# Who makes the remainders of the second expert weights: GpSimd's and VectorE's shares redrawn in a metaformer block

## The reference

```
x = x + conv_attention(layernorm(x))         # q, k, v; softmax along rows plus softmax along columns; Wo
t = layernorm(x) as 2048 tokens
expert of a token = argmax of softmax(t @ wg); its place = how many came before it; 256 places each
h = relu(dispatched[e] @ w1[e])              # 256 x 256 by 256 x 1024, eight experts
y = h @ w2[e]                                # 256 x 1024 by 1024 x 256
x = x + gate * y, put back at the token
```

## Time and profile before

| | before |
|---|---|
| median of 3 runs | 187.49 us (187.36 to 187.66) |
| the profiled execution | 187.47 us, its span 185.5 us |
| TensorE busy | 176.2 us, 95% of the span |
| VectorE busy | 142.3 us, 77% |
| GpSimd busy | 120.7 us, 65% |
| ScalarE busy | 113.6 us, 61% |

### The profile page before, as it was taken

One profiled execution on the slowest core, in us unless ns is written; L12 is line 12 of the kernel. 1 busy time (PEld: TensorE's weight loads), 2 busy tenths in 40 slices (PEclk: granted clock), 3 DMA queues, 4 the chain that ended last, 5 costly groups with the idle time before them and its releaser, 6 DMA issues.

```text
span 185.5 us, 3928 instructions
## 1 busy us (share of the span) xinstructions
PE 176.2 (95%) x1372; PEld 169.5 (91%) x1372; DVE 142.3 (77%) x394; ACT 113.6 (61%) x275; POOL 120.7 (65%) x156
## 2 busy tenths in 40 slices
PE   7999999999999999999999979999999999999980
PEld 7998999999989997779999969999999999999970
DVE  0697749889998899763557899699996998995820
ACT  3348776968859787715578990691953955827000
POOL 4267264787888988579237599538587196369552
PEclk9999999999999999999999999999999999999997
DMA  5897996731111329392999129257166192261010
GB/s 171 240 391 223 321 241 168 277 117 59 62 59 57 111 71 310 102 349 99 265 339 306 43 68 393 77 189 266 58 223 255 58 345 112 44 208 47 4 69 28
DMA packets 23860, 31.66 MB, mean 171 GB/s; under 512 B 2728, under 2 KB 20649, under 8 KB 23840
## 3 DMA queue, kind: packets, MB, share of 16 engines
q1 hardware_dynamic: 21264, 26.32, 43.9%
q0 software_dynamic: 1616, 4.24, 6.4%
q10 hardware_dynamic: 960, 0.85, 1.4%
HBM read 23.02 MB, written 8.55 MB: 170 GB/s over the span
## 4 chain that ended last, share of the span: by engine, by line
PE 70%; DVE 14%; ACT 4%; DMA 3%; issue 3%; POOL 3%; POOLq 1%; SPq 0%; DVEq 0%; ACTq 0%
PE banks_v L634 7%; PE banks_v L635 7%; PE banks_v L641 7%; PE banks_o L706 5%; PE bank_pT L634 4%; PE bank_pT L641 4%; PE bank_pT L635 4%; PE bank_q L641 3%; DMA sl<-in_x 3%; PE bank_s L641 3%; PE bank_q L634 3%; PE bank_q L635 3%; PE bank_s L634 3%; PE bank_s L635 3%; DVE qT_low L1165 2%
## 5 line engine op out<-in xcount | busy, mean ns | idle before, releaser
L984 ACT ACTIVATE w_high<-w_in_sb 128x1024 fp32r<-128x1024 f32 x22 | 22.9, 1058 | 6.4 <-DMA w_in_sb<-in_L_ffn_w 6.4
L573 POOL TENSOR_TENSOR w_low<-vx,w_high 128x1024 fp32r<-128x1024 f32 x8 | 20.5, 2579 | 8.3 <-ACT w_high L984 8.3
L591 POOL DMA_INDIRECT out<-y,goal x16 | 16.7, 1044 | 12.9 <-DVE y L1386 6.0
L1364 DVE TENSOR_TENSOR w_low<-w_in_sb,w_high 128x1024 fp32r<-128x1024 f32 x12 | 16.1, 1339 | 5.8 <-ACT w_high L984 5.7
L573 POOL TENSOR_TENSOR w_low<-w_in_sb,w_high 128x1024 fp32r<-128x1024 f32 x7 | 16.7, 2399 | 5.8 <-ACT w_high L984 5.8
L506 POOL DMA_INDIRECT slots<-row,slot x14 | 14.4, 1027 | 6.7 <-DVE slot L1277 3.3
L706 PE MATMUL banks_o<-vx,pT 128*128 128x266 f32 x64 | 16.5, 397 | 0.2 <-issue 0.2
L634 PE MATMUL banks_v<-w_high,h_high 128*128 128x256 f32 x64 | 16.1, 288 | 0.0
L635 PE MATMUL banks_v<-w_high,h_low 128*128 128x256 f32 x64 | 15.7, 283 | 0.0
L1085 ACT ACTIVATE h_high<-bank_xT 128x512 fp32r<-128x512 f32 x8 | 4.7, 593 | 17.3 <-PE bank_xT L641 17.3
L634 PE MATMUL bank_pT<-w_high,h_high 128*128 128x256 f32 x56 | 14.0, 288 | 1.3 <-POOL w_low L573 1.3
(11 more groups left out here) (245 smaller groups left out, 656.8 us busy)
## 6 DMA issues: line engine op xcount, KB each, us to landing
w_in_sb<-in_L_ffn_w SPq DMA_DIRECT2D x12, 1024.0 KB, 7.5
vx<-in_L_ffn_w SPq DMA_DIRECT2D x4, 1024.0 KB, 5.6
sl<-slots SPq DMA_DIRECT2D x9, 266.0 KB, 4.5
slots<-empty SPq DMA_DIRECT2D x8, 266.0 KB, 4.3
sl<-in_x SPq DMA_DIRECT2D x8, 256.0 KB, 7.1
out<-row SPq DMA_DIRECT2D x7, 256.0 KB, 2.1
table_in<-in_tables SPq DMA_DIRECT2D x1, 292.0 KB, 6.0
w_in_sb<-in_L_conv_Wk SPq DMA_DIRECT2D x1, 256.0 KB, 3.4
```

Source lines behind the costliest of these rows:

```text
L573: step = nc.gpsimd.tensor_tensor(w2_low[e % 2][:, half, :], w2_raw[e % 2][:, half, :], w2_high[e % 2][:, half, :].bitcast(f32), ALU.subtract)
L591: nc.gpsimd.indirect_dma_start(out_rows, bass.IndirectOffsetOnAxis(ap=goal[j][:, c:c + 1].bitcast(u32), axis=0), y[j][:, c, :], None, boun ...
L984: nc.scalar.activation(high[e % 2][:, half, :], raw[:, half, :], ACT.Copy).then_inc(ready, 1)
L1364: step = nc.vector.tensor_tensor(w1_low[e % 2][:, c, :], w1_in_sb[:, c, :], w1_high[e % 2][:, c, :].bitcast(f32), ALU.subtract)
```

## The change

The program no longer has GpSimd make any remainder of w2: VectorE makes them all, in halves of 128x1024, at places of its order given below. The four quarters of the second expert's w1 (L515), which GpSimd made in turns 4, 5 and 6, are made behind its six last scatters. SP's load of the third expert's w1, which needs them done, moves from the attention (L389, L390) to behind the slot loads of experts 1, 0, 2 and 3. The semaphore `first_w2_low` goes away, with the waits on it.

```diff
-W1_LOW = {4: (0,), 5: (1,), 6: (2, 3)}
...
             for i in (last, EARLY):
                 sp.wait_ge(x2_ready, 2 * i + 2)
                 sp.dma_start(out_view[:, tiles(i), :], row[i % 2][:, :, 0:D]).then_inc(x2_stored[i % 2], 16)
-            sp.wait_ge(w1_split, 2)
-            sp.dma_start(w1_in_sb[:, :, :], w1_view[2]).then_inc(w1_in, 16)
...
             for e in range(2, E):
+                if e == 4:
+                    sp.wait_ge(w1_split, 2)
+                    sp.dma_start(w1_in_sb[:, :, :], w1_view[2]).then_inc(w1_in, 16)
                 load_slots(e)
             sp.sem_inc(y_free, 2)
...
                 sp.wait_ge(w2_split, e - 1)
-                if e == 2:
-                    sp.wait_ge(first_w2_low, 1)
...
                 x_and_bias(i)
-                for n in W1_LOW.get(i, ()):
-                    second_w1_low(n)
...
             scatter_rows(B - 1)
-
-            def split_w2(e, parts):
-
-                for part in parts:
-                    pool.wait_ge(w2_high_ready, 2 * e + part + 1)
-                    half = slice(part * FC // 2, (part + 1) * FC // 2)
-                    step = nc.gpsimd.tensor_tensor(w2_low[e % 2][:, half, :], w2_raw[e % 2][:, half, :], w2_high[e % 2][:, half, :].bitcast(f32), ALU.subtract)
-                if part == 1 or e == 0:
-                    step.then_inc(w2_split, 1)
+            for n in range(4):
+                second_w1_low(n)
...
-            split_w2(0, [0])
             slot_rstd(1, 1)
             slot_rstd(0, 2)
-            split_w2(1, [0])
             slot_rstd(2, 3)
...
             scatter_y(0)
-            split_w2(1, [1])
             slot_rstd(3, 4)
             for e in range(1, E - 1):
-                split_w2(e + 1, range(2))
...
                 pe.wait_ge(w2_split, e + 1)
-                if e == 0:
-                    pe.wait_ge(first_w2_low, 1)
-                else:
+                if e:
                     pe.wait_ge(h_split, (FC // 2) * (e + 1))
...
-            first_w2_piece(2)
-            first_w2_piece(3).then_inc(first_w2_low, 1)
+            def split_w2(e, which=range(2)):
+
+                for part in which:
+                    dve.wait_ge(w2_high_ready, 2 * e + part + 1)
+                    half = slice(part * FC // 2, (part + 1) * FC // 2)
+                    step = nc.vector.tensor_tensor(w2_low[e % 2][:, half, :], w2_raw[e % 2][:, half, :], w2_high[e % 2][:, half, :].bitcast(f32), ALU.subtract)
+                if part == 1:
+                    step.then_inc(w2_split, 1)
+
+            split_w2(0, [0])
 
             for c in range(DC):
                 dve.wait_ge(x0_high_ready, c + 1)
                 step = nc.vector.tensor_tensor(xg_low[0][:, c, :], ps_x0[c], xg_high[0][:, c, :].bitcast(f32), ALU.subtract)
             step.then_inc(xg_split, 1)
-            hidden_low(0, [0])
-            hidden_low(0, [1, 2, 3])
+            split_w2(0, [1])
+            hidden_low(0, range(FC // 2))
+            split_w2(1, [0])
             gathered(1)
...
             output_rows(0, 2)
             hidden_low(1, [3])
+            split_w2(1, [1])
             for e in range(1, E - 1):
...
                 if e + 2 < E:
                     gathered_low(e + 2)
+                split_w2(e + 1)
                 output_rows(e, 1 if e == 1 else e + 1)
```

More of the change, by code:

```diff
@@ L245, in build @@
         w1_high_ready, w1_split, w2_high_ready, w2_split = (sem(n) for n in ("w1_high_ready", "w1_split", "w2_high_ready", "w2_split"))
-        first_w2_low = sem("first_w2_low")
         row_free, y_free = sem("row_free"), sem("y_free")
@@ L1331, in _ @@
             nc.vector.tensor_copy(slot_of(B - 1)[:, :], place_of[1][:, :]).then_inc(slot_ready, 1)
[L1333 to L1337, removed]
             def slot_shift(e):
```

## The result

| | before | after |
|---|---|---|
| median | 187.57 us (4 runs, 187.36 to 188.87) | 192.65 us (4 runs, 192.46 to 193.27) |
| ratio | | 1.0269, 95% interval 1.0236 to 1.0303 |
| the profiled execution: time, span | 187.47, 185.5 us | 192.46, 190.7 us |
| mean granted clock | 0.993 | 0.978 |
| last block of matmuls starts | 179.03 us | 184.10 us |

The change costs 5.1 us. The forecast was 192.1 us, with a range of 189.5 to 194.2.

The account below looks back on a forecast made before the run. The prediction took TensorE to bound the kernel, with no idle time in the expert stage. Its sum was 187.47 + 3.87 (later second hidden product) − 1.33 (gap gone) + 2.1 (clock) = 192.1 us, range 189.5 to 194.2.

Parts of the forecast that it names:

- The bound: Expert stage: TensorE has no idle time, so faster VectorE or GpSimd is worth nothing; only TensorE's standing still counts.
- The attention gives back 1.1: Attention: without the four pieces VectorE is no longer held, and TensorE gets back 0.88+0.21 = 1.1 us.
- Pieces, and the issue at 89.8: Behind the last scatters: four GpSimd pieces run from 84.77 to 89.75, then SP issues the load at about 89.8.
- Landing in 6.2 us: Third expert's w1 load: 6.2 us from issue, as in the attention, so landed at 96.0 (95.1 to 97.9).
- Who waits: ScalarE works in order, so expert 1's copy waits for the load; second hidden product starts 2.7 us behind landing, at 98.7.
- The stall: Ahead of the second hidden product: TensorE stands still for 4.97 us, from 93.73 to 98.7.
- The w2 remainders cost nothing: Expert loop: VectorE's two added w2 pieces per expert cost nothing under TensorE's full stretch; 2.46 us per expert without cover.
- The gap's return: Ahead of the second expert's output product: TensorE's gap of 1.33 us, ended by GpSimd's remainder, is gone.
- The rival's order: VectorE's first expert 1 piece runs before GpSimd's fourth, 1.2 us later: 193.3 us; later-load rivals together had 0.16.
- Late next: Fourth expert's first weight: loaded at 101.8 in place of 97.9, landed by 109.9, first multiplied at 117, so hidden.
- The clock: Behind the stall: TensorE restarts at 1.2 GHz, costing 2.1 us; rival that the clock stays up, 190.0 us, had 0.15.
- The sum: Whole kernel: 187.47 + 3.87 − 1.33 + 2.1 = 192.11 us, the 1.1 from the attention already in the 3.87.

Follow-up runs that it names:

- roundings in between: Changed kernel, load behind two slot loads, VectorE making half the second w1's remainder, third expert's roundings behind expert 0's squares and expert 1's first hidden copy: 187.04 us, ratio 0.9952.
- pieces alone: Kernel before with only GpSimd's four pieces and the third expert's w1 load moved, GpSimd keeping its w2 share: 194.04 us, ratio 1.033.
- w2 part alone: Changed kernel with the four pieces and the third expert's w1 load back in the attention as they were: 185.90 us, ratio 0.9899.
- nothing behind the load: Changed kernel with SP waiting for the moved load to land before the last four slot loads: 192.87 us, ratio 1.0291.
- two slot loads ahead: Changed kernel with the moved load issued behind two slot loads in place of four: 190.66 us, ratio 1.0163.

## Why the prediction came out right, step by step

**The bound.** Right. VectorE and GpSimd lost 6.7 and 34.0 us of busy time and gave nothing by that; only the places where TensorE stood still moved the time.

**The attention gives back 1.1.** It gave 1.30, with all three held ops at 0.16. The first hidden product starts at 80.73 to 81.60 us in nine profiles without the pieces in the attention (the kernel after's among them, roundings in between left out), and at 82.34 and 82.82 in the two with them.

**Pieces, and the issue at 89.8.** Four pieces from 84.95 to 89.99 (84.77 to 89.75 predicted), issue at 90.01. The 0.2 comes from one scatter of 1.33 us for 0.97. VectorE was at a remainder from 81.60 to 82.82 beside it. That scatter takes 1.32 to 1.35 us in all ten traces with this remainder, and 0.97 in the two without it, the kernel before and the pieces alone:

```profile
82.02 0.97 POOL L507 DMA_INDIRECT slots<-row_last,slot_last  x1 [0.30 <-issue]
```

The two always come together, but no run moved the remainder by itself.

**Landing in 6.2 us: the mis-sized term.** It took 7.7. I took the load of the attention as the nearest row because the slot loads ahead would be "partly done". The runs put a size on that: 4.8 to 5.0 us when those ahead had landed or were within 0.2 us of it, 6.9 to 7.7 behind four of which the last had not, 8.3 directly behind two that had just been issued. Taking away what follows it gave 7.0, within that spread.

**Who waits.** Right in each step: 2.7 us from landing to the second hidden product were predicted, and 97.7 to 100.40 is 2.7. Moving the roundings behind the copy took 6.2 us off the median (192.65 to 186.47), all but 1.27 us of idleness.

**The stall.** 4.97 predicted, 6.70 measured: 1.5 of the difference is the landing, 0.2 the issue.

**The w2 remainders cost nothing.** Right, by the w2 part alone. The gap's return was 1.6 us, not 1.33: the idle time that the row names is not all of it. Where the other 0.26 lies, no run says. The rival's order with VectorE ahead of GpSimd's fourth piece did not come, though its condition did. I had taken it that VectorE runs first once its piece is ready before the third of GpSimd's ends. It was ready at 88.55, and the fourth started at 88.71 all the same; VectorE was held instead, with no one waiting for it (timeline of VectorE, kernel after):

```profile
88.55 2.53 DVE L1372 TENSOR_TENSOR w_low<-vx,w_high 128x1024 fp32r<-128x1024 f32 x1
```

That is the mutual stop of the page "SBUF — State Buffer" of the Trainium skill (section on who interferes with whom), seen from the other side: the piece took 2.53 us, where the same form at 81.60 took 1.22. By the order of issue, which the rival took over from that section of the Trainium skill, VectorE would have come ahead of the fourth piece; this row does not bear that out.

**Late next.** Right. The fourth w1 is issued at 103.51, 1.7 us later than predicted with the landing, and TensorE has no idle time there.

**The clock.** Right in kind: the clock fell in the stall and the product restarted slowly. It took 1.4 us in this trace, not 2.1, and the 2.1 was not a size of this stall. I priced it by the first matmuls of the kernel (4.63 us for 20 of 128 columns, at twice the later spacing, though the stretch view has the granted clock at 1.00 there). What the runs show in its place: the price is what of the low stretch falls on matmuls, 3.2 us here, 4.6, 5.7 and 3.4 in three versions, for 1.4, 2.0, 2.6 and 1.6 us. The run with extra matmuls shows the term apart: clock at 1.00 throughout, and 0.1 us in its place. The Trainium skill ("TensorE: Matmul & The Clock Gate", section on HAM oscillation) has it that each long wait is paid anew; the stalls of 3.83 to 6.70 us here agree. The one of 1.27 us, with the clock at 1.00 from 93 to 106 us, paid nothing.

**The sum.** Predicted −1.1 + 4.97 + 2.1 − 1.33 = +4.64, measured −1.30 + 6.70 + 1.40 − 1.59 = +5.21. The stall was 1.7 too small, the clock 0.7 too large, and the two gains together 0.5 too small. Being near was in part luck, these errors cancelling; the clock's term was lucky too, since between versions of this kernel it moved from 1.4 to 2.6 us.

## What to carry to other kernels

When a load moves behind other work, find the first instruction on every engine that reads it and ask what stands behind that in its order: here 1 us of rounding, needed by no one until the third product, held the copy for the second and cost some 6 us. Price the load by what is in flight ahead of it at the issue, not by its size or by the same load elsewhere; a later issue behind landed transfers can land earlier. A stall of several us on TensorE cost its length and 1.4 to 2.6 us of restart at half clock besides. Balancing two engines that don't bound the kernel was worth nothing.

## What the runs showed of the hardware

- **The same 1 MB load took 4.8 to 8.3 us on one queue, by what was ahead.** Four slot loads of 266 KB ahead and not all landed: 6.9, 7.0, 7.7. Two or four landed, or within 0.2 us of it: 4.8, 4.9, 4.9, 5.0. Directly behind two just issued: 8.3, twice. In the 7.0 us case the DMA share was 0.16 and 0.14 from 95 to 97 us, ahead of the landing at 97.6: by estimate some 2.5 of the 16 DMA engines were busy on the average. Which, and why, no run asked. "Not landed" is not the whole measure either. In the kernel before, the load issued at 97.89 took 5.3 us, though the w2 load ahead of it (issued at 91.83, 8.0 us by the DMA view) landed only at 99.8.
- **The clock's price did not follow the length of the stall, but where the low stretch lay.** The longest stall was the cheapest: there the clock fell 3.1 us behind TensorE's last matmul and half of the low stretch passed in idleness, while in the others it fell 3.8 to 4.4 us behind it. The time at 0.50 behind the restart, times (1 − 0.12/0.21), gives 1.4, 2.0, 2.5 and 1.5 us, which is the price by the marks to within 0.1. What sets the moment of the fall, and why the low stretch was shorter in the last, no run asked.

| version | TensorE idle | clock at 0.50, about | of it behind the restart | price by the marks |
|---|---|---|---|---|
| after | 6.70 us | 96.8 to 103.6 us | 3.2 us | 1.4 us |
| nothing behind the load | 6.06 | 98.1 to 104.9 | 4.6 | 2.0 |
| pieces alone | 5.51 | 98.2 to 105.0 | 5.7 | 2.6 |
| two slot loads ahead | 3.83 | 97.9 to 101.3 | 3.4 | 1.6 |

- **An idle time in a row is not all that a stall costs.** The gap of 1.33 us was worth 1.59, and the stall of 0.98 us at 100.96 cost 1.6 (transposes of expert 2 to those of expert 3: 9.18 us against 7.62), some 0.25 of it a second, shorter wait for the low part behind it.
